# Queries of two batches and keys of the second made beside the first sparse layer's tiles, with one PSUM bank a product, and GpSimd's bias and residual put behind the rotation

## The reference, cut to what matters

```
x += lru(LN(x))          # per 512-row chunk (two a batch): three input products, complex scan over
                         # time, mid product, gelu MLP, layer norm
x += sparse_ffn(LN(x))   # conv features -> batch norm over all rows -> gelu -> two 256-wide logits;
                         # softmax limited to the 32 largest of each row gates the 256x256 product,
                         # once on its output ("full") and once on its input ("inner")
x += attention(LN(x))    # 8 heads of 64, queries against latent keys of 64, softmax over the whole
                         # batch (1024 keys), weighted sum of the latent, output product
x += sparse_ffn(LN(x))
```

## Time and profile before

| | |
|---|---|
| runs | 1419.39, 1422.08, 1425.52 us; median 1422.08 |
| profiled execution | 1419.8 us, span 1418.1 |
| busy in the span | PE 1219.2 (86%), DVE 1183.4 (83%), ACT 1094.3 (77%), POOL 992.4 (70%) |
| mean granted TensorE clock | 0.962 |
| the chain that ended last | PE 43%, DVE 22%, issue 17%, ACT 13%, POOL 4% |
| issues | x loads x8, 512 KB, 3.9 us; rows of the maxima x64, 1 KB, 1.9 us |

### The profile page before, as it was taken

How to read it: one execution, slowest core, us unless ns; L and a number is a source line. 1 busy time by engine, 2 the same in 40 slices (tenths; PEclk the granted TensorE clock), 3 DMA queues, 4 the chain that set the end, 5 groups by cost and what they waited for, 6 DMA issues and landing times.

```text
span 1418.1 us, 30913 instructions
## 1 busy us (share of the span) xinstructions
PE 1219.2 (86%) x10172; PEld 746.1 (53%) x10172; DVE 1183.4 (83%) x3173; ACT 1094.3 (77%) x2471; POOL 992.4 (70%) x1129
## 2 busy tenths in 40 slices
PE   4999989757677679999999999999999999667776
PEld 2455445434444335565666666666666667344443
DVE  7999999489999988777787778877878854799997
ACT  3332333688899679999999998999998994898886
POOL 4356753368788867767877677787777874398887
PEclk9999999989999999999999999999999999799997
DMA  6200000000000000000000000000000000000000
GB/s 169 74 1 1 0 0 1 1 1 1 1 1 1 1 1 2 2 3 2 2 2 2 2 2 2 2 2 2 2 2 2 2 2 1 1 31 16 31 16 31
DMA packets 27067, 14.84 MB, mean 10 GB/s; under 512 B 15062, under 2 KB 26652, under 8 KB 26908
## 3 DMA queue, kind: packets, MB, share of 16 engines
q1 hardware_dynamic: 26908, 12.87, 3.5%
HBM read 8.60 MB, written 4.19 MB: 9 GB/s over the span
## 4 chain that ended last, share of the span: by engine, by line
PE 43%; DVE 22%; issue 17%; ACT 13%; POOL 4%; DVEq 0%; DMA 0%; SPq 0%; POOLq 0%; ACTq 0%
PE banks L1848 6%; PE banks L1850 5%; DVE arena L1385 5%; PE banks L1837 5%; DVE arena L1380 4%; ACT arena L1056 4%; PE banks L1798 4%; PE banks L1774 3%; PE banks L1866 3%; PE banks L1865 3%; PE banks L1867 3%; ACT arena L1064 2%; DVE arena L1244 2%; DVE arena L1227 2%; POOL arena L726 2%
## 5 line engine op out<-in xcount | busy, mean ns | idle before, releaser
L726 POOL TENSOR_TENSOR arena<-arena 128x512 f16<-128x512 f32 x384 | 440.6, 1164 | 156.9 <-ACT arena L1064 152.1
L1056 ACT ACTIVATE arena<-banks 128x512 f32<-128x512 f32 x512 | 304.3, 600 | 53.8 <-PE banks L1850 49.9
L1459 DVE TENSOR_REDUCE arena<-banks 128x1 f32<-128x512 f32 x512 | 327.2, 679 | 9.5 <-PE banks L1837 6.4
L1064 ACT ACTIVATE arena<-arena 128x512 f16<-128x512 f32 x512 | 316.3, 633 | 0.0
L1865 PE MATMUL banks<-arena 128*128 128x65 f16 x2048 | 214.4, 193 | 6.1 <-POOL arena L726 5.8
L1866 PE MATMUL banks<-arena 128*128 128x64 f16 x2048 | 214.5, 195 | 0.0
L1867 PE MATMUL banks<-arena 128*128 128x65 f16 x2048 | 213.6, 192 | 0.0
L1483 DVE TENSOR_TENSOR arena<-arena 128x512 f16<-128x512 f32 x128 | 106.3, 830 | 125.0 <-ACT arena L1064 124.6
L1865 PEld LDWEIGHTS banks<-arena 128*128 128x128 f16 x2048 | 190.9, 96 | 35.3 <-issue 9.3
L1385 DVE MATCH_REPLACE8 arena<-arena 128x256 f32<-128x256 f32 x512 | 205.8, 409 | 1.1 <-issue 0.8
L1848 PE MATMUL banks<-arena 128*128 128x512 f16 x512 | 194.1, 379 | 14.2 <-ACT arena L1056 12.3
(11 more groups left out here) (200 smaller groups left out, 2681.8 us busy)
## 6 DMA issues: line engine op xcount, KB each, us to landing
x<-in_L_attn_a_x SPq DMA_DIRECT2D x8, 512.0 KB, 3.9
out<-x SPq DMA_DIRECT2D x8, 512.0 KB, 2.9
arena<-arena SPq DMA_DIRECT2D x64, 1.0 KB, 1.9
arena<-in_L_attn_a_W_in SPq DMA_DIRECT2D x1, 768.0 KB, 5.7
arena<-in_L_attn_a_W_mid SPq DMA_DIRECT2D x1, 512.0 KB, 7.4
arena<-in_L_attn_a_w_w SPq DMA_DIRECT2D x2, 256.0 KB, 7.7
arena<-in_L_attn_b_Wq SPq DMA_DIRECT2D x1, 512.0 KB
arena<-in_L_attn_b_Wo SPq DMA_DIRECT2D x1, 512.0 KB
```

Of the source, the lines that this page charges most:

```text
L726: nc.gpsimd.tensor_tensor(pr_lo[c][:, kt, :], pr[:, kt, :], pr_hi[c][:, kt, :], ALU.subtract).then_inc(a_lP, 1)
L1056: nc.scalar.activation(pr[:, kt, :], ps[6 + kt % 2][:, :], ACT.Exp, scale=SM_SCALE).then_inc(a_P, 1)
L1064: nc.scalar.activation(pr_hi[c][:, kt, :], pr[:, kt, :], ACT.Copy).then_inc(a_hi, 1)
L1459: nc.vector.tensor_reduce(mx_half[c][:, i // 2, i % 2:i % 2 + 1], ps[n % MAX_BANKS][:, :], X, ALU.max).then_inc(a_mx, 1)
```

## The change

In the recurrent stage GpSimd's first chunk and each step have a wait for the whole rotation (`turned_whole`) ahead of residual and bias, and the bias comes ahead of the roots. In both sparse layers one z row a tile in a ring of four serves both uses, the gelu is taken in place, so that no copy of its tile is made, the full product has bank 5 alone and the inner one bank 6, and ScalarE copies sparse x and the full product before the logits. The head now makes keys and latents of batches 0 and 1 and all their queries, 16 chunk products of four heads' pairs, by a new table of (what, chunk, part, bank). A high part is copied by ScalarE, subtracted in PSUM by a product with minus the identity, and the low part copied again by ScalarE. Queries go to device memory (`q_store`) by DMA and come back by head. In the attention batches 0 and 1 make no queries, and batch 0 prepares nothing for batch 1. The diff, cut to its core:

```diff
+Z_RING = 4
+AHEAD = 2
...
-        HEAD_ROWS_AT = {8 + r: r for r in range(2 * TPC)}
-        HEAD_TURN_AT = {12: (0, 0), 13: (0, 1), 16: (1, 0), 17: (1, 1)}
-        HEAD_KEYS_AT = {18: 0, 20: 1}
-        HEAD_LATENT_AT = {22: 0, 24: 1}
-        HEAD_QUERY_AT = {26: 0, 28: 1}
-        HEAD_STATS_AT = {6: 0, 10: 1}
+        HEAD_STATS_AT = {6: 0, 10: 1, 14: 2, 18: 3}
+        HEAD_ROWS_AT = {8: (0, 1), 9: (2, 3), 12: (4,), 13: (5,), 14: (6, 7), 16: (8,), 17: (9,), 18: (10,), 19: (11,),
+                        21: (12,), 22: (13,), 23: (14,), 24: (15,)}
+        HEAD_AT = {
+            9: (("turn", 0, 0, 2), ("turn", 0, 1, 3)),
+            10: (("keys", 0, None, 7),),
+            11: (("query", 0, 0, 7), ("latent", 0, None, 3)),
+            12: (("query", 0, 1, 7),),
+            13: (("query", 0, 2, 7),),
+            14: (("query", 0, 3, 7), ("turn", 1, 0, 2), ("turn", 1, 1, 3)),
+            15: (("keys", 1, None, 7),),
+            16: (("query", 1, 0, 7), ("latent", 1, None, 3)),
+            17: (("query", 1, 1, 7),),
+            18: (("query", 1, 2, 7),),
+            19: (("query", 1, 3, 7), ("turn", 2, 0, 2), ("turn", 2, 1, 3)),
+            20: (("keys", 2, None, 7),),
+            21: (("query", 2, 0, 7),),
+            22: (("query", 2, 1, 7), ("latent", 2, None, 3)),
+            23: (("query", 2, 2, 7),),
+            24: (("query", 2, 3, 7), ("turn", 3, 0, 2), ("turn", 3, 1, 3)),
+            25: (("keys", 3, None, 7),),
+            26: (("query", 3, 0, 7), ("latent", 3, None, 3)),
+            27: (("query", 3, 1, 7), ("query", 3, 2, 2)),
+            28: (("query", 3, 3, 7),),
+        }
...
+            at, onward = (w, slot), AHEAD <= B + 1 < BATCH
...
-                    if at in QUERY_AT and (w < 12 or onward) else
+                    if at in QUERY_AT and (B >= AHEAD if w < 12 else onward) else
...
+            def store(k, G):
+                B, c = k // 2, k % 2
+                rows = q_store[:, B, 2 * G:2 * G + 2, :, c * CH:c * CH + CH].rearrange("s h d t -> s (h d) t")
+                sp.wait_ge(h_qlo, k * GROUPS + G + 1)
+                for part in range(2):
+                    sp.dma_start(rows[part], staged[(k % 2) * GROUPS + G][:, part, :]).then_inc(s_qst[k], 16)
+            def load(head):
+                B, hh, slot = head // NH, head % NH, head % Q_RING
+                if head % NH == 0:
+                    for k in (2 * B, 2 * B + 1):
+                        sp.wait_ge(s_qst[k], 2 * GROUPS * 16)
+                wait_from(sp, s_qld, head * 48)
+                wait_from(sp, a_sps, (head - Q_RING + 1) * 2 * KT)
+                for half in range(2):
+                    sp.dma_start(qA[HD * half:HD * half + HD, slot, :], q_store[0, B, hh]).then_inc(s_qld, 16)
+                sp.dma_start(qB[0:HD, slot, :], q_store[1, B, hh]).then_inc(s_qld, 16)
+            for k in range(2 * AHEAD):
+                for G in range(GROUPS):
+                    store(k, G)
+                if k == 1:
+                    for head in range(Q_RING):
+                        load(head)
...
+                if W % 2 and Q_RING <= (W - 3) // 2 + Q_RING < AHEAD * NH:
+                    load((W - 3) // 2 + Q_RING)
...
+            def turned_whole(n):
+                pool.wait_ge(l_dve, n * L_STEPS + L_STEPS)
...
+            turned_back(0, 0)
+            turned_back(0, 1)
+            rstd(2, 2)
+            turned_whole(0)
             add_ln_bias(0)
-            turned_back(0, 0)
-            rstd(2, 2)
-            turned_back(0, 1)
-            add_ln_bias(1)
             def lru_step(n, c, behind, ahead1, ahead2, ahead4):
                 if ahead1:
@@ -617,14 +688,16 @@
                     rstd2(n - 1)
                 if ahead1:
                     turned_back(n + 1, 1)
+                    turned_whole(n + 1)
                 if behind:
                     residual(n - 1)
                 if n == 0:
+                    add_ln_bias(1)
                     rstd(3, 3)
+                if ahead2:
+                    add_ln_bias(n + 2)
                 if ahead4:
                     rstd(n + 4, n + 4)
-                if ahead2:
-                    add_ln_bias(n + 2)
                 if behind:
                     next_rstd((n - 1) * TPC, n - 1, TPC)
...
-            def ffn_zs(f, t, p):
+            def ffn_z(f, t):
                 T = t + f * NT
-                if not (isinstance(T, int) and T < 2):
-                    act.wait_ge(f_s, T - 1)
-                    act.sem_inc(s_turn, 1)
-                z_tile(t, zs[p]).then_inc(f_zs, 1)
+                wait_from(act, f_s, T - Z_RING + 1)
+                z_tile(t, zf[t % Z_RING]).then_inc(f_z, 1)
...
-                    ffn_z(f, p, p)
-                    ffn_zs(f, p, p)
+                    ffn_z(f, p)
...
+                    gelu(t * P, P).then_inc(f_g01, 1)
+                gelu(2 * P, CH - 2 * P).then_inc(f_xa_all, 1)
+                for n in range(1, NCH):
+                    gelu(n * CH, CH).then_inc(f_xa_all, 1)
...
-                    ffn_z(f, t + 2, q)
-                    ffn_xa(f, t + 2, q)
+                    ffn_z(f, t + 2)
                     ffn_rest(f, t, q)
+                    if f == 0:
+                        head_first(t)
                     ffn_zT(f, t + 2, q)
                     ffn_exp(f, t + 1, 1 - q)
+                    ffn_sT(f, t, q)
+                    ffn_fs(f, t, q)
                     ffn_logits(f, t + 2, q)
                     if f == 0:
-                        head(t)
-                    ffn_sT(f, t, q)
-                    ffn_fs(f, t, q)
-                    ffn_zs(f, t + 2, q)
+                        head_second(t)
                     ffn_gs(f, t, q)
...
+            def head_first(t):
+                for what, k, part, bank in HEAD_AT.get(t - 1, ()):
+                    B, c = k // 2, k % 2
+                    if what == "turn":
+                        turned(B, c, part, bank)
+                    if what == "keys":
+                        cs = slice(c * CH, c * CH + CH)
+                        act.wait_ge(a_kps, k + 1)
+                        nc.scalar.activation(kA[B][:, cs], ps[bank][:, :], ACT.Copy).then_inc(h_khi, 1)
+                        nc.scalar.activation(kB[B][0:HD, cs], ps[bank][0:HD, :], ACT.Copy).then_inc(h_khi, 1)
+                    if what == "latent":
+                        latent(B, c, bank)
+                    if what == "query":
+                        n = k * GROUPS + part
+                        if k > 1 and part == 0:
+                            act.wait_ge(s_qst[k - 2], 2 * GROUPS * 16)
+                        act.wait_ge(h_qps, n + 1)
+                        nc.scalar.activation(staged[n % (2 * GROUPS)][:, 0, :], ps[bank][:, :],
+                                             ACT.Copy).then_inc(h_qhi, 1)
+            def head_second(t):
+                for what, k, part, bank in HEAD_AT.get(t - 1, ()):
+                    B, c = k // 2, k % 2
+                    if what == "keys":
+                        act.wait_ge(h_kmps, k + 1)
+                        nc.scalar.activation(kA[B][HD:P, c * CH:c * CH + CH], ps[bank][HD:P, :],
+                                             ACT.Copy).then_inc(a_kl, 1)
+                    if what == "query":
+                        n = k * GROUPS + part
+                        act.wait_ge(h_qmps, n + 1)
+                        nc.scalar.activation(staged[n % (2 * GROUPS)][:, 1, :], ps[bank][:, :],
+                                             ACT.Copy).then_inc(h_qlo, 1)
+                for r in HEAD_ROWS_AT.get(t, ()):
+                    attn_row(r // (2 * TPC), r % (2 * TPC))
             ffn(0)
             max_scaled(0)
@@ -1103,7 +1182,7 @@
                                 latent(n, part, bank)
                     if kt == 3 and W + 1 < ALL:
                         max_scaled(W + 1)
-                    if (w, kt) in ROWS_AT and B + 1 < BATCH:
+                    if (w, kt) in ROWS_AT and AHEAD <= B + 1 < BATCH:
...
             def ffn_full(f, t, p):
                 T = t + f * NT
                 pe.wait_ge(f_zT, T + 1)
-                pe.wait_ge(f_fs, T - 1 + CREDIT["f_fs"])
+                pe.wait_ge(f_fs, T + CREDIT["f_fs"])
                 for k in range(KB2):
-                    last = mm(ps[(2, 5)[p]][:, 0:D], zfT[p][:, k, :], fW[:, k, :], start=k == 0, stop=k == KB2 - 1)
+                    last = mm(ps[5][:, 0:D], zfT[p][:, k, :], fW[:, k, :], start=k == 0, stop=k == KB2 - 1)
                 last.then_inc(f_fps, 1)
...
                 T = t + f * NT
-                pe.wait_ge(f_gs, T - 1 + CREDIT["f_gs"])
...
-                        head(t)
+                        head_second(t)
                     ffn_in(f, t, t % 2)
+                    if f == 0:
+                        head_first(t)
...
+            def head_first(t):
+                for what, k, part, bank in HEAD_AT.get(t, ()):
+                    B, c = k // 2, k % 2
```

(34 more changed lines are left out.)

135 lines of the change are left out of this document (50 added, 85 removed).

## The result

The changed kernel takes **1384.24 us** (median of 4 runs, 1379.71 to 1386.57), the kernel before 1422.24 in the same comparison: ratio 0.9728, 95% interval 0.9702 to 0.9754. The prediction was 1377 with a range of 1363 to 1399. The profiled execution after has a span of 1384.9 us against 1418.1; it was the slowest of its four, and the one before lies 2.4 us under its median.

A forecast was written before the change was run, and what follows sets the result against it. Each stage was taken to have another bound: VectorE in the sparse layers, TensorE in the attention, TensorE waiting in gaps in the recurrent stage. 1419.8 - 28 - 11 + 3 + 0.5 - 7 = 1377 us, range 1363 to 1399.

The forecast's parts named there:

- the second layer: Second sparse layer: VectorE is the bound, logits come after two more copies in the first tiles; plus 0.5 us.
- Batch 0, -28: Attention of batch 0: without queries and preparation, all 16 pieces take 8.55 us, 136.8 in all; minus 28 us.
- The rival that batch 0 stays tied to GpSimd's low halves: Attention of batch 0: pieces don't reach 8.55 us; 11 us more, 1388 us in all, chance 0.1.
- Batch 1, -11: Attention of batch 1: six queries of 1.72 us go, with a little of the duplicates' waits; minus 11 us.
- TensorE is 98% busy: Attention of batch 1: step pricing six removed queries at their full 1.72 us each, 10.3 us.
- The first sparse layer, +3: First sparse layer: query tiles take 6.26 us against VectorE's 5.82, sum 204.9 against 200.5; plus 3 us.
- the chain through the bank and the query: First sparse layer: inner product, bank 7 wait, query, full product, z turned, copy, exponentials; 6.26 us a query tile.
- Recurrent stage, -7: Recurrent stage: GpSimd waits for the rotation, so TensorE's gaps of 3.59 and 1.73 us and 2 us of others close; minus 7.
- the milder rival: Recurrent stage gives nothing: GpSimd's second product meets VectorE's second scan, up to 2.36 us a chunk; 1384 us, chance 0.07.
- my bounds (minus 10): Recurrent stage: bounds of the term, 0 and minus 10 us.
- Loads, minus-identity products, single banks: nothing: Query loads, first sparse layer's 20 minus-identity products, and one bank each for full and inner products: 0 us each.
- The slower rival: Sparse layers: single bank ties full product to scaled copy, 0.86 us in each of 64 tiles; 55 us, 1432, chance 0.04.

The follow-up runs named there:

- banks and spread statistics: The changed kernel with the head's products rotated over banks 2, 3 and 7 and each statistics group spread over four tiles: 1377.50 us.
- new banks: The changed kernel with the head's products rotated over banks 2, 3 and 7: 1377.42 us.
- no minus-identity products: The changed kernel without the first sparse layer's 20 minus-identity products, low-half copies kept but multiplied by 0: 1384.76 us.
- product once: The changed kernel with TensorE's products of the six queries put back into batch 0, results unread: 1392.21 us.
- rows: The changed kernel with ScalarE's eight rows of layer norm put back into batch 0 at their old places: 1387.77 us.
- last queries one a tile: The changed kernel with rotated banks, statistics spread over four tiles a group, and the last three queries one each in tiles 27 to 29: 1376.13 us.
- spread statistics: The changed kernel with the four tiles of a statistics group taken one in each of four tiles (3 to 18): 1384.47 us.
- duplicates: The changed kernel with twelve of GpSimd's 64x512 copies put back into batch 0, on scratch: 1390.29 us.
- no rows in batch 1: The changed kernel without the eight rows of layer norm ScalarE makes in batch 1 for batch 2: 1383.62 us.
- loads twice: The changed kernel with every load of queries from device memory made twice: 1382.85 us.
- product twice: The changed kernel with each half of the six queries' products made twice in batch 0, results unread: 1401.61 us.

## Why the prediction came out as it did

It was right in sign, size and order of the terms, 7 us too low in the median. In the profiled pair the terms add up to -42.5 and measured -33.3, 9.2 short: 6.8 in the first sparse layer, 4.2 in batch 1 and 0.2 at the start, less 1.3 that batch 0 and 0.7 that the second layer gave on top. In the medians the drop is 38.0, as the changed kernel's profiled execution was its slowest: part of the closeness is luck.

1. **Batch 0, -28 for -29.3.** Right: all pieces from the third on at the floor of 8.55. The reason was right in kind and too narrow: products (7.4 us alone), duplicates (6.0) and rows (2.4) each hold pieces up, no one of them alone, and 13.5 us were not taken apart. The rival that batch 0 stays tied to GpSimd's low halves failed: no wait of TensorE for them is left, and putting the duplicates back brings one of 1.6 us.
2. **Batch 1, -11 for -6.8.** The step that failed is "TensorE is 98% busy", so that a query is worth its full 1.72 us. Of the 10.3 us taken out, TensorE's busy time in the batch lost 9.0 (166.39 to 157.38), and its idle time grew by 2.2 (2.90 to 5.10): its waits for exponentials went from 1.6 to 2.6 us and those for maxima from 0.8 to 1.9. In batch 0 the doubled product shows that pieces hold 0.43 us of room which the busy share hides, and that a product beside a piece is worth 1.29. Six are 7.7, near the 6.8, but that nearness is in part chance: the six pieces of batch 1 that lost a query became 2.10, 0.96, 0.63, 1.57, 1.13 and 0.73 us shorter. What holds each of them was not tried; the run there shows only that ScalarE's rows are not it. The Trainium skill ("Perfetto Trace Analysis", Identifying the Most-Contended Engine) says that matmul busy time is a poor measure, as matmuls are pipelined. The trace agrees that it is one, 8.46 us busy with 8.12 us of work, but not in direction: by the page pipelined matmuls look smaller in the trace, and here they look larger.
3. **The first sparse layer, +3 for +9.8.** The mechanism was right: the chain through the bank and the query, with MAX8 waiting for the logits. The term was mis-sized in two places. Tiles 10 to 28 took 128.2 us, not 123.6: the query started 1.90 us after the copy where I had 1.7, a tile was 6.39 to 6.67 where I had 6.26. And the last three took 17.7 us, where two steps of 5.82 and a last one of 2.94 are 14.6, because the doubled tile's copies hit the tile behind it (the spread of the last queries won 1.8 of that). The wait for bank 7 was in my chain as 0.3 us a tile, some 5.5 us in all, and was a little larger: taking it away gave 6.9 us over 19 tiles.
4. **Recurrent stage, -7 for -6.8.** The number is right and half of its reason is not. I read the gain off one pair of scans, but the scans as a sum got nothing; the milder rival ("GpSimd reaches its second product just when VectorE reaches the second scan") happened in three chunks. The 12 us came from the rotations and sums, which I had not looked at. The waits of TensorE that I read the term from (3.6 and 1.7 us) are gone, with one of 1.3; but VectorE was the engine that set the stage, busy 205.95 of 211.40 us from 20 us to the last scans before and 196.03 of 201.51 after, and its 9.9 us are the whole gain. The stage itself won 9.9 us, at the edge of my bounds (minus 10), and 3.1 were lost again behind the last scans. That the two make -7 is luck.
5. **Loads, minus-identity products, single banks: nothing**, right. The doubled loads, the left-out products and the second layer's tiles (186.9 us busy of 190.1) show it. The slower rival, a full product tied to the scaled copy in each tile, did not appear: in the second layer, which has the single banks and no head work, the reciprocals take 180.9 us from first to last against 180.8.

## What to carry to other kernels

Before pricing an item at its full length because an engine is 98% busy, look for the same engine's room: put the item in twice, and the difference between the first and the second is the room. When several users share one buffer in a ring of one, look at who reads it last; rotating three banks that were already there was worth 7 us, where leaving out 20 products was worth nothing. A slow tile in one engine's row is no proof of a cost, since the next tiles can be shorter for it: compare sums over the stretch.

## What was not expected of the hardware

**GpSimd and VectorE.** A 128x1024 VectorE operation with two SBUF inputs lasts 1.21 us alone and 1.97 as the mean of the group that GpSimd's additions to x fell on, and those last 2.9 instead of 2.0 us. Timeline of GpSimd before, residual and bias:

```profile
177.79 2.91 POOL L565 TENSOR_TENSOR x<-x,arena 128x1024 f32<-128x1024 f32 x1
180.66 2.91 POOL L550 TENSOR_TENSOR x<-x,arena 128x1024 f32<-128x1024 f32 x1
```

Before, GpSimd worked beside VectorE's rotations and scans; after, it waits for the rotation (9.49 us in the chunk shown) and the stage is 9.9 us shorter. Doing the side work later, in one place, beat doing it as early as it could be done.

**The clock.** Up to the last scans (221.4 to 221.6 us) eleven of the twelve executions with this recurrent stage agree within 0.17 us; in the twelfth, banks and spread statistics, they start at 223.2. Its granted clock from 45 to 55 us was 0.83, where the kernel after has 1.00, with TensorE busy for 9.95 of the 10 us in both and for 6.60 of 6.70 just before the fall. The first reciprocal then comes anywhere from 288.3 to 292.8 us. The executions fall into three groups by the granted clock (a mean of its two levels, 2.4 and 1.2 GHz) in two windows:

| clock, 215 to 225 us | 250 to 260 us | last scans to first reciprocal | kernels |
|---|---|---|---|
| 0.84 to 0.87 | 0.83 | 71.0 to 71.3 us | the kernel after, new banks, no minus-identity products, product once, rows, last queries one a tile |
| 1.00 | 0.83 | 69.3 to 69.7 | spread statistics, duplicates, no rows in batch 1 |
| 1.00 | 1.00 | 66.8 to 67.8 | loads twice, product twice, banks with spread statistics |

What TensorE did before the first fall is the same in the groups: at 222.1 it has waited 2.42 us for ScalarE. Then the same four products follow, in the kernel after and in the one with doubled loads:

```profile
222.11 1.98 PE L1651 MATMUL banks<-zT,conv 128*64 128x512 f32 x4 [2.42 <-ACT zT L851]
222.12 1.08 PE L1653 MATMUL banks<-zT,conv 128*64 128x512 f32 x4 [2.42 <-ACT zT L853]
```

The second fall follows a wait of 1.82 us for ScalarE, which ends at 252.59 in the kernel after. So the groups, with the same code in this stretch, differ by up to 4.5 us, and the earlier falls of the clock go with the longer ones. Before the change the clock is 1.00 from 215 to 260 us and the stretch is 68.1 us. So some 3 of the 9.9 us that the stage won were given back in the profiled execution and not in all. Why the clock fell in one and not in the other stays open.
